# Output projection as fp32 products instead of three products of fp16 halves

## What is computed

```python
x = x + attention(layernorm(x))     # 32 heads of 16, causal; ends in  out @ Wo.T + bo
x = x + ffn(layernorm(x))           # dequantised weights, 512 -> 1792 -> 512
x = x + topk_mlp(layernorm(x))      # silu gate, the smallest half of 1376 set to zero
x = x + ffn(layernorm(x))           # the same weights again
```

## Time and profile before

| | |
|---|---|
| median of 3 runs | 2203.8 us (2194.07 to 2206.63) |
| the profiled execution | 2189.01 us, of which 2187.2 us are its span |
| PE busy | 2021.1 us, 92% of the span |
| DVE busy | 1543.5 us, 71% |
| ACT busy | 1022.0 us, 47% |
| output projection, from its first loads to the next phase's first load | 766.4 to 826.6 us |

### The profile page before, as it was taken

How to read it: one execution, slowest core, us unless ns; L and a number is a source line. 1 busy time by engine, 2 the same in 40 slices (tenths; PEclk the granted TensorE clock), 3 DMA queues, 4 the chain that set the end, 5 groups by cost and what they waited for, 6 DMA issues and landing times.

```text
span 2187.2 us, 38402 instructions
## 1 busy us (share of the span) xinstructions
PE 2021.1 (92%) x14288; PEld 1234.7 (56%) x14288; DVE 1543.5 (71%) x2736; ACT 1022.0 (47%) x1658; POOL 558.7 (26%) x587
## 2 busy tenths in 40 slices
PE   5887999999999887899999999999999979889989
PEld 2342344444444345677677677677677555556656
DVE  6775677777777341289688597696696898989841
ACT  3221456656566521265364364373463564646511
POOL 2224354644342241012112012012012111121221
PEclk9997899999999988999999999999999999999999
DMA  7766234533233072110310400500400403031000
GB/s 258 236 220 175 67 99 117 139 88 83 76 84 93 19 244 110 55 50 1 108 49 1 154 23 1 175 1 1 174 2 14 152 1 132 24 113 53 11 11 10
DMA packets 115656, 187.35 MB, mean 86 GB/s; under 512 B 43200, under 2 KB 68176, under 8 KB 115520
## 3 DMA queue, kind: packets, MB, share of 16 engines
q1 hardware_dynamic: 91344, 133.22, 19.6%
q0 software_dynamic: 9088, 32.12, 5.1%
q10 hardware_dynamic: 15088, 20.19, 2.6%
HBM read 151.59 MB, written 33.62 MB: 85 GB/s over the span
## 4 chain that ended last, share of the span: by engine, by line
PE 46%; DVE 12%; issue 3%; ACT 1%; POOL 0%; DVEq 0%; ACTq 0%; POOLq 0%
PE ga L1364 10%; PE acc L1374 10%; PE ub L1364 10%; DVE junk L1534 7%; PE ga L1392 5%; PE ub L1392 5%; PE acc L1417 4%; DVE pat L1538 2%; DVE h L1591 1%; PE d_tr L1213 1%; DVE T L1540 1%; DVE lohi L1606 1%; PE d_tr L1403 0%; DVE X L1616 0%; DVE d_xn L1200 0%
## 5 line engine op out<-in xcount | busy, mean ns | idle before, releaser
L842 DVE TENSOR_REDUCE mx<-s 128x1 f32<-128x512 f32 (+3 forms) x608 | 380.8, 661 | 125.7 <-PE s L731 72.3
L1465 ACT ACTIVATE junk_a<-ax,T 128x1376 f16<-128x1376 f32 x248 | 357.8, 1443 | 200.8 <-DVE T L1540 195.1
L823 ACT ACTIVATE pr<-s 128x1024 f32<-128x1024 f32 (+3 forms) x352 | 301.2, 869 | 240.3 <-PE s L750 178.4
L1534 DVE TENSOR_SCALAR_CACHE_REDUCE junk<-ax,T 128x1376 f16<-128x1376 f32 x248 | 406.8, 1640 | 3.5
L1326 POOL TENSOR_TENSOR lohi<-h,lohi 128x256 f16<-128x256 f32 x224 | 172.7, 771 | 871.9 <-ACT lohi L1476 871.5
L1364 PE MATMUL ga<-xT_f,w_gate 128*128 128x256 f16 x2688 | 336.3, 276 | 38.4 <-DVE h L1591 35.3
L1364 PE MATMUL ub<-xT_f,w_up 128*128 128x256 f16 x2688 | 333.1, 274 | 0.0
L1364 PEld LDWEIGHTS ga<-xT_f,w_gate 128*128 128x128 f16 x2688 | 261.8, 99 | 121.1 <-DVE h L1591 54.7
L1374 PE MATMUL acc<-w_down,lohi 128*128 128x512 f16 x1344 | 326.1, 379 | 2.8 <-DVE X L1616 2.8
L1364 PEld LDWEIGHTS ub<-xT_f,w_up 128*128 128x128 f16 x2688 | 264.9, 99 | 32.4
L728 PE MATMUL s<-K,Q 65*128 65x512 f16 (+3 forms) x768 | 244.8, 344 | 26.0 <-DMA K<-onerow 12.9
(11 more groups left out here) (142 smaller groups left out, 2407.2 us busy)
## 6 DMA issues: line engine op xcount, KB each, us to landing
ring<-wgu_scr SPq DMA_DIRECT2D x64, 688.0 KB, 5.0
ring<-wd_scr SPq DMA_DIRECT2D x24, 768.0 KB, 4.7
wgu_scr<-tk_h POOLq DMA_DIRECT2D x16, 344.0 KB, 6.1
q_scr<-qk_h ACTq DMA_DIRECT2D x16, 256.0 KB, 4.0
k_scr<-qk_h ACTq DMA_DIRECT2D x16, 256.0 KB, 2.5
v_scr<-v_f ACTq DMA_DIRECT2D x16, 256.0 KB, 3.5
Q<-q_scr SPq DMA_DIRECT2D x32, 128.0 KB
K<-k_scr SPq DMA_DIRECT2D x32, 128.0 KB
```

The costliest lines, as they stand in the source:

```text
L823: nc.scalar.activation(pr[:, kb % 2, j0:j1, 0:w], scores, ACT.Exp, scale=SCALE).then_inc(e2_ok, 1)
L842: nc.vector.tensor_reduce(dst, s1[u % 2][:, 0:(j1 - j0) * w].rearrange("p (j k) -> p j k", k=w), AX.X, ALU.max).then_inc(r1_ok, 1)
L1465: nc.scalar.activation(junk_a[:, :], ax[k % 2][:, 1, :], ACT.Sign, scale=-1.0, bias=TF[:, 1:2], accum_out=cnt[:, 1:2]).then_inc(c1_ok, 1)
L1534: nc.vector.tensor_scalar(junk[:, :], ax[k % 2][:, 0, :], TF[:, 0:1], -float(KZERO), ALU.is_lt, ALU.add, accum_out=cnt[:, 0:1]).then_inc(c ...
```

## The change

Wo is loaded straight into an fp32 tile `w`, and the transposed rows are copied to an fp32 `c_oT`. The split of Wo, the low part of the rows and the scale factors are gone. A tile's product is four fp32 matmuls (`k` = 0 to 3) where there were twelve fp16 ones. The first product waits for each piece of Wo as it lands. DVE's addition is a plain add of PSUM and `cX`. The order of transposes and products is the same. The declarations, cut, and then the code:

```diff
-        w_raw = sb("wo_raw", [P, KB, D], F32)
-        w = sb("wo", [P, 2, KB, D], F16)
+        w = sb("wo", [P, KB, D], F32)
...
-        oT = sb("c_oT", [P, 2, 2, KB, P], F16)
+        oT = sb("c_oT", [P, 2, KB, P], F32)
...
@@ -1025,20 +1021,18 @@
         def _(pe):
             def transposes(t, h, i):
                 pe.wait_ge(o_ld[i], 16 * (h + 1))
-                wait(pe, lo_ok, t - 1)
+                wait(pe, oT_ok, t - 1)
                 for k in range(KB):
                     tr = nc.tensor.transpose(ptr[i][:, k, :], o_in[:, i, k * P:(k + 1) * P], ident[:, :])
                 tr.then_inc(tr_ok, 1)
 
             def product(t, i):
-                pe.wait_ge(lo_ok, t + 1)
+                pe.wait_ge(oT_ok, t + 1)
                 wait(pe, x_ok, t - 1)
-                ops = [(a, k, b) for k in range(KB) for a, b in ((0, 0), (0, 1), (1, 0))]
-                for n, (a, k, b) in enumerate(ops):
-                    if isinstance(t, int) and t == 0 and n % 3 == 0:
-                        pe.wait_ge(w_lo, k + 1)
-                    mm = nc.tensor.matmul(pmm[i][:, :], oT[:, i, a, k, :], w[:, b, k, :], start=(n == 0),
-                                          stop=(n == len(ops) - 1))
+                for k in range(KB):
+                    if isinstance(t, int) and t == 0:
+                        pe.wait_ge(w_ld[k], 16)
+                    mm = nc.tensor.matmul(pmm[i][:, :], oT[:, i, k, :], w[:, k, :], start=(k == 0), stop=(k == KB - 1))
                 mm.then_inc(mm_ok, 1)
             transposes(0, 0, 0)
             for h in first_then_loop(pe, NT // 2 - 1):
@@ -1053,8 +1047,9 @@
         @block.scalar
         def _(act):
             for k in range(KB):
-                act.dma_start(w_raw[:, k, :], WoT[k * P:(k + 1) * P, :]).then_inc(w_ld[k], 16)
+                act.dma_start(w[:, k, :], WoT[k * P:(k + 1) * P, :]).then_inc(w_ld[k], 16)
             act.dma_start(bo_all[:, :], bo.unsqueeze(0).broadcast_to([P, D])).then_inc(b_ld, 16)
+
             def store(t):
                 act.wait_ge(x_ok, t + 1)
                 act.dma_start(x1_scr[t * P:(t + 1) * P, :], X[:, t, :]).then_inc(x1_st, 16)
@@ -1062,11 +1057,7 @@
             for t in range(NT):
                 act.wait_ge(tr_ok, t + 1)
                 wait(act, mm_ok, t - 1)
-                nc.scalar.activation(oT[:, t % 2, 0, :, :], ptr[t % 2][:, :, :], ACT.Copy, scale=OS).then_inc(hi_ok, 1)
-                if t == 0:
-                    for k in range(KB):
-                        act.wait_ge(w_ld[k], 16)
-                        nc.scalar.activation(w[:, 0, k, :], w_raw[:, k, :], ACT.Copy, scale=WS).then_inc(w_hi, 1)
+                nc.scalar.activation(oT[:, t % 2, :, :], ptr[t % 2][:, :, :], ACT.Copy).then_inc(oT_ok, 1)
                 if t >= 2:
                     store(t - 2)
             store(NT - 2)
@@ -1075,31 +1066,16 @@
 
         @block.vector
         def _(dve):
-            def lo(t, i):
-                dve.wait_ge(hi_ok, t + 1)
-                nc.vector.scalar_tensor_tensor(out=oT[:, i, 1, :, :], in0=ptr[i][:, :, :], scalar=OS,
-                                               in1=oT[:, i, 0, :, :], op0=ALU.mult, op1=ALU.subtract).then_inc(lo_ok, 1)
-
             def add(t, i):
                 dve.wait_ge(mm_ok, t + 1)
                 dve.wait_ge(xb_ok, t + 1)
                 xt = X[:, bass.ds(t, 1), :] if not isinstance(t, int) else X[:, t:t + 1, :]
                 xt = xt.rearrange("p o d -> p (o d)")
-                nc.vector.scalar_tensor_tensor(out=xt, in0=pmm[i][:, :], scalar=1.0 / (OS * WS), in1=xt,
-                                               op0=ALU.mult, op1=ALU.add).then_inc(x_ok, 1)
-            lo(0, 0)
-            for k in range(KB):
-                dve.wait_ge(w_hi, k + 1)
-                nc.vector.scalar_tensor_tensor(out=w[:, 1, k, :], in0=w_raw[:, k, :], scalar=WS, in1=w[:, 0, k, :],
-                                               op0=ALU.mult, op1=ALU.subtract).then_inc(w_lo, 1)
-            for h in first_then_loop(dve, NT // 2 - 1):
-                lo(2 * h + 1, 1)
+                nc.vector.tensor_tensor(xt, pmm[i][:, :], xt, ALU.add).then_inc(x_ok, 1)
+
+            for h in first_then_loop(dve, NT // 2):
                 add(2 * h, 0)
-                lo(2 * h + 2, 0)
                 add(2 * h + 1, 1)
-            lo(NT - 1, 1)
-            add(NT - 2, 0)
-            add(NT - 1, 1)
 
 
 def phase_mlp(nc, ident, w_gate, w_up, w_down, wgu_scr, wd_scr, x1_scr, out):
```

More of the change, by code:

```diff
@@ L983, in phase_output @@
         w_ld = [sem(f"wo_in{k}") for k in range(KB)]
-        w_hi = sem("wo_hi")
-        w_lo = sem("wo_lo")
         x_ld = [sem(f"cx_in{n}") for n in range(2)]
@@ L990, in phase_output @@
         tr_ok = sem("ctr_ok")
-        hi_ok = sem("chi_ok")
-        lo_ok = sem("clo_ok")
+        oT_ok = sem("coT_ok")
         mm_ok = sem("cmm_ok")
```

## The result

The changed kernel takes 2212.28 us, median of 22 runs (2197.92 to 2225.15). The kernel before takes 2197.14 us in 22 runs of the same sessions (2186.63 to 2207.63). The ratio is 1.0056, with a 95% interval of 1.0036 to 1.0075. That is 12 us, between 8 and 16: slower, by about the 0.5% that can just be told from no change. The means of the runs (2210.5 and 2198.2 us) give that ratio; the two medians lie 15.1 us apart.

The account below looks back on a forecast made before the run. PE was taken to bound the output projection. Fifteen products, 15 x (3.44 - 2.59) = +12.75 us, with +0.3 at the start and nothing at the end, gave +13.0 on the median 2203.8: 2217 us, range 2204 to 2226.

Parts of the forecast that it names:

- PE sets the pace of the stage: Output projection's steady part: PE is the bound at 3.03 us a tile; removing ACT or DVE work there gives nothing.
- One fp32 matmul of 512 columns is two records and 0.86 us: Product of each projection tile: four fp32 matmuls take 3.44 us against 2.59, so a tile lasts 3.88 us, not 3.03.
- Loads at nothing: Weight loads before the projection's fp32 matmuls: 141 ns each, run ahead under the matmuls, costed at nothing.
- The start, +0.3 us,: Projection's first product: starts at 772.3 without the split, ends at 778.6 against 778.30; range -1.6 to +0.8 us.
- The end, at nothing,: Projection's last add, store and block end, after the last two products: nothing changes but the product before.
- The sum: Whole kernel: +12.75 us from the fifteen products after the first, +0.3 at the start, nothing at the end: +13.0 us.
- The level: Base time of the whole kernel: the difference is added to the runs' median of 2203.8 us, giving 2217 us.
- Rival 1: Projection's fp32 product is cheaper, not slower; reloading row buffers then bounds a tile at 2.5 us; 2194 us, chance 9%.

Follow-up runs that it names:

- The removal alone: The kernel before with its twelve fp16 matmuls kept, all on high parts, and no low parts made; stage 59.16 us, period 3.03 us a tile.

## Why the prediction was right

- *PE sets the pace of the stage* held. PE's idle time is 0.0 us on either side, and taking half of DVE's work away left 3.03 us a tile.
- *One fp32 matmul of 512 columns is two records and 0.86 us.* Measured 0.857 (0.429 a record), from neighbours that were column groups at one place and transposes at the other. Doubling it confirmed it. This term made the result: predicted 15 x 0.85 = 12.75 us, measured 15 x 0.851 = 12.76. The Trainium skill's four passes ("FP8 and Floating Point Precision", section TensorE Precision Notes) would make the product 1.33 times as long; 3.43 to 2.59 is 1.32. Its halved rate for FP32_LOW_HIGH ("Perfetto Trace Analysis", section Engine Utilization) agrees with the trace only if it is read of each of the two records, 0.429 us against 0.216; the whole matmul takes four times as long.
- *Loads at nothing* held, but by an argument that was too timid and with a wrong figure. I expected loads of about 141 ns; they take 190. At records four times shorter they remain almost free, 0.14 us a tile.
- *The start, +0.3 us,* was the term that was mis-sized: -1.4 us, near the best case (-1.6). Product 0 started 5.7 us after the first load, close to the 5.9 that I had put, but took 4.82 us and not 6.3. I had let the clock rise where it rose before, at 11.7 us after the first load, when product 0 was over; it rose after about 8.4, in the middle of the product. The removal alone gave -1.1 us, with the clock rising after about 8 us; how much of either is the split and how much the clock was not separated.
- *The end, at nothing,* was +0.1 us.
- *The sum* was +13.0 and came to +11.4 in the stage. The whole measured 12 us by the ratio of the runs.
- *The level* was the weakest part. I had seen that three runs and a profile spread over 17 us, and added the difference to a median of 2203.8 that later became 2197.14. That put the level 6.7 us too high. The medians then differed by 15.1 us and not 13.0, so the two errors partly cancelled, by luck, and 2217 lies 4.7 us above the measured 2212.28. The cause of the scatter stood in the trace of before, in the windows of attention's start, which I had not read.
- *Rival 1's price* was wrong, though the rival did not come. The row buffers alone were to bound a cheap product at 2.5 us a tile. It came out at 2.99: rows landed after 4.8 us and not 4.4, the loads of x had a part in it, and the clock fell back in between, which I had not thought of. With both kinds of loads issued earlier it was 2.0, about what the full DMA engines allow.

## What to carry to other kernels

Count a matmul in start distances, never in record lengths, and price an fp32 one at four fp16 ones: a split into three fp16 products wins as long as TensorE is the bound and the split is hidden beside it. Work that is taken off engines which wait is worth what it did at the stage's start, here 1 us of 60. When a change moves 0.5%, compare its stage in the two traces and the granted clock ahead of it before believing two totals.

## What the runs showed of the hardware

- An fp32 matmul of 128 rows by 128 columns of weights and 512 moving columns left two records, 0.429 us each from start to start, where an fp16 one takes 0.216.
- An fp32 weight load before a product took 190 to 192 ns, before a transpose 141, before an fp16 matmul 98. At record starts 0.112 us apart the 192 ns loads still cost almost nothing (0.14 us for a tile's 32).
- The granted clock stayed at 0.50 from attention's start until about 240 us in one execution and 271 us in another, while PE was busy for 86 to 100% of the windows shown above (203 to 240 us, and 240 to 270). The later rise put the next stage 15.5 us later in a 2200 us kernel.
- Full clock at attention's first matmul (197 us) did not last: it was 0.50 from about 203 us on, where PE waits for DVE between units. One or two filling matmuls a unit held it, and it fell 1.5 to 5 us after they ended.
- A DMA load of 256 KB took 4.4 us to land with the engines 70 to 90% busy and 7.2 us with them 92 to 104% busy (790 to 810 us) and loads issued three tiles ahead.
